# A two-layer convolution kernel on one core: ScalarE's root for the first statistics, and ScalarE's copies of the first two streams' weights placed earlier

## The chip, the cores and the metric

The kernel runs on one core of one Trainium2 chip. The metric is the device time of one execution in microseconds, the median of several runs; the runs of one kernel shown here lie within 0.3% of each other.

## The reference

The input `x` is (16, 32, 48, 48). Two residual layers follow each other; each normalises in 16 groups of two channels per image, convolves, and adds:

```python
def _gn(v, G=16, eps=1e-05):
    g = v.reshape(B_, G, C_ // G, H_, W_)
    m = jnp.mean(g, axis=(2, 3, 4), keepdims=True)
    s = jnp.var(g, axis=(2, 3, 4), keepdims=True)
    return ((g - m) / jnp.sqrt(s + eps)).reshape(v.shape)
...
x = x + _L0_conv_ref(_gn(x), L0_conv_weight, L0_conv_bias)   # 9x9, zero padding
x = x + _L1_conv_ref(_gn(x), L1_conv_weight)                 # 5x5, reflect padding
```

The 9x9 kernels of the first layer are Gaussians made from three parameters for each pair of channels (two widths and an angle): `exp(-0.5 q)` divided by its own sum over the 81 taps. The 5x5 kernels of the second layer are given.

## The kernel before, in words

**Tiling.** The 128 partitions hold 4 neighbouring image rows of 32 channels. Images go in pairs (8 pairs, `n`), and layer 1 works on quads of four images (4 quads, `qd`). Vertically both convolutions are done in transformed form: layer 1 forms 8 streams `s(i)`, linear combinations of normalised row blocks, multiplies each by its own weights `i` with TensorE (nine horizontal taps), and combines the 8 products into output rows; layer 2 does the same with 4 streams and five taps. Each float32 operand is split into two float16 parts, `hi` and `lo` for streams, `wh` and `wl` for weights, so a product is three rows of matmuls: `wh*hi`, `wh*lo`, `wl*hi` (`conv1`, lines 1454 to 1482). ScalarE makes every `hi` and `wh` by a copy (`high_half`, `high_kernel`, `high_kernel_two`), VectorE every `lo` and `wl` by a subtraction that has to wait for that copy (`low_half`, `low_kernel`).

**Order of the work.** Every engine runs a list written out by hand, in order, and engines meet through semaphores alone. On VectorE the list is `first_quad()` and what follows it, on ScalarE the calls from line 1228 on, on TensorE the calls from line 1556 on. An instruction that waits holds up everything behind it on its engine.

**The first quad.** Nothing can be multiplied until the Gaussian weights and the first statistics exist. VectorE makes the exponents (`exponents`), ScalarE takes them through `Exp` (`kernel_exponentials`, line 1174), VectorE adds blocks of them (`outer_blocks`, `all_blocks`, `tap_pairs`, `kernel_sum`) and scales the weights of stream 1 by the reciprocal of the sum (line 884). Between these steps VectorE computes 1/sqrt(var+eps) of the first four images from `vare` in its own arithmetic: a guess from the bits of the float (`first_guess`), a Newton step (`first_newton`), and a second step of higher order (`second_root`, `first_scales`), which gives the scale `gsc` and the offset `gof`. These small operations have 4 elements per partition.

Streams 1 and 2 of the first quad take a short cut: TensorE forms them from the raw `x` (`near_rows`, with three scaled identity matrices from `near_factors`), ScalarE applies scale and offset for stream 1 (`first_stream1`) and VectorE the scale for stream 2 (`first_stream2`). The other streams need the four normalised images, which ScalarE writes to `P1` (`normalise1`, two instructions an image). TensorE then goes through `FIRST_PARTS`: for each stream a part with the five taps that were "made" and a part with the four "turned" taps, mirror images of the taps of another stream. For streams 1 and 2 TensorE turns partitions itself (`turn_partitions`, line 1527) and ScalarE copies the result (`turned_kernel`); for the rest ScalarE copies (`turn_kernel`) and DMAs from SP's queue move the partitions (line 408).

**Later statistics** (`small_stats`, line 650) use ScalarE for the root: VectorE writes `vare`, ScalarE gives `std` (`standard_deviation`, line 1102), VectorE takes the reciprocal and one Newton step. ScalarE's functions live in tables that an `ACT_TABLE_LOAD` instruction brings in; the program has three, for `Sin` (line 1229), `Exp` (line 1231) and `Sqrt` (line 1278). The last stands just ahead of the `hi` copy of the last stream of the first quad (stream 6) and of the second quad's root.

Of the kernel before, what the change touches and what calls it, by code (L numbers as in the profile page):

```python
# [26 lines left out]
ALU = mybir.AluOpType  # L27
ACT = mybir.ActivationFunctionType
# [4 lines left out]
I32 = mybir.dt.int32  # L33
# [46 lines left out]
X_SCALE = 64.0  # L80
# [10 lines left out]
NF = len(OUT_FACTORS)  # L91
EPS = 1e-5
ROUND = 12582912.0
ROOT_BITS = float(0x5F3759DF + 6 * 2**23)
ROOT3 = 0.375 ** 0.5
TWO_PI = 6.2831850
SMALL = 9

# [53 lines left out]
def build(nc, x, w0, bias, w1, tables, out):  # L152
    with ExitStack() as ctx:
# [182 lines left out]
        def block1(b):  # L336
            return ker[:, :, b * P:(b + 1) * P]
# [46 lines left out]
        MARK = {}  # L384
# [53 lines left out]
        def _(dve):  # L438
# [71 lines left out]
            def outer_blocks(part):  # L510
                dve.wait_ge(exp_done, part + 1)
                at = slice(*EXP_PARTS[part])
                done(tt(slot(2)[:, at, :], block1(0)[:, at, :], block1(2)[:, at, :], ALU.add))
                MARK["outer blocks", part] = count[0]

            def all_blocks(part):
                dve.wait_ge(dve_w, MARK["outer blocks", part])
                at = slice(*EXP_PARTS[part])
                done(tt(slot(1)[:, at, :], slot(2)[:, at, :], block1(1)[:, at, :], ALU.add))
                MARK["all blocks"] = count[0]  # L520
# [77 lines left out]
            def step(ins):  # L598

                step_count[0] += 1  # L600
                ins.then_inc(first_step_done, 1)

            def step_landed():
                dve.wait_ge(first_step_done, step_count[0])
# [10 lines left out]
            def first_variance():  # L615
                dve.wait_ge(stat_mm, 1)
                step_landed()
                step(tt(var[1][:, :], STAT[1][:, QI:], msq[1][:, :], ALU.add))
                step_landed()
                step(ts(vare[1][:, :], var[1][:, :], 0.0, EPS, ALU.max, ALU.add))  # L620

            def first_guess():
                step_landed()
                step(ts(rcp[1][:, :].bitcast(I32), vare[1][:, :].bitcast(I32), -0.5, ROOT_BITS, ALU.mult, ALU.add))
                step_landed()
                step(stt(msq[1][:, :], vare[1][:, :], -0.5 / (X_SCALE * X_SCALE), rcp[1][:, :], ALU.mult, ALU.mult))

            def first_newton():
                step_landed()
                step(tt(var[1][:, :], msq[1][:, :], rcp[1][:, :], ALU.mult))  # L630
                step_landed()
                step(stt(rcp[1][:, :], var[1][:, :], 1.5, rcp[1][:, :], ALU.add, ALU.mult))

            def second_root():

                step_landed()
                step(stt(msq[1][:, :], vare[1][:, :], ROOT3 / (X_SCALE * X_SCALE), rcp[1][:, :], ALU.mult, ALU.mult))
                step_landed()
                step(tt(var[1][:, :], msq[1][:, :], rcp[1][:, :], ALU.mult))

            def first_scales():
                step_landed()
                step(stt(msq[1][:, :], var[1][:, :], -1.25 / ROOT3, var[1][:, :], ALU.add, ALU.mult))
                step_landed()
                stt(gsc[1][:, :], msq[1][:, :], 1.875, rcp[1][:, :], ALU.add, ALU.mult).then_inc(small[1], SMALL - 2)
                dve.wait_ge(small[1], SMALL - 2)
                stt(off1[:, :], first_mean, -NEAR_OFFSET, gsc[1][:, :], ALU.mult, ALU.mult).then_inc(small[1], 1)
                stt(gof[1][:, :], first_mean, -1.0, gsc[1][:, :], ALU.mult, ALU.mult).then_inc(small[1], 1)

            def small_stats(c, n):  # L650
# [10 lines left out]
                tt(var[c][:, :], ex2, msq[c][:, :], ALU.add).then_inc(small[c], 1)  # L661
                dve.wait_ge(small[c], at + 3)
                ts(vare[c][:, :], var[c][:, :], 0.0, EPS, ALU.max, ALU.add).then_inc(small[c], 1)
                dve.wait_ge(std_done[c], n + 1 if c == 2 else n)
                nc.vector.reciprocal(rcp[c][:, :], std[c][:, :]).then_inc(small[c], 1)

                dve.wait_ge(small[c], at + 5)
# [194 lines left out]
            def first_quad():  # L862
# [7 lines left out]
                outer_blocks(0)  # L870
                first_variance()
                all_blocks(0)
                first_guess()
                outer_blocks(1)
                first_newton()
                all_blocks(1)
                second_root()
                tap_pairs()
                first_scales()
                kernel_sum()  # L880
# [5 lines left out]
                kernel_scale()  # L886
                low_half(1, 0, 0)
                scaled(block1(1), "block1")
                first_stream2()
                low_kernel(1)  # L890
                made_two()
                low_half(1, 0, 1)
                low_kernel(2)
# [182 lines left out]
        def _(act):  # L1076
# [156 lines left out]
            near_factors((0,))  # L1233
            channel_sums(1, 0, range(2, 4))
            kernel_exponentials()
            near_factors((1, 2))
            opposite_rows()
            first_stream1()
            high_half(1, 0, 0)
            normalise1(0, range(2))  # L1240
            high_kernel(1)
            normalise1(0, range(2, 3))
            high_half(1, 0, 1)
            high_kernel_two()
            turned_kernel(1, 0)
            normalise1(0, range(3, 4))
            turned_kernel(1, 1)
# [26 lines left out]
            turn_kernel(5, wh)  # L1274
            high_kernel(6)
            turn_kernel(5, wl)

            nc.scalar.activation(warm[:, :], bias_c[2][:, :], ACT.Sqrt)
            high_half(1, 0, 7)
            standard_deviation(1, 1)  # L1280
            turn_kernel(6, wh)
# [339 lines left out]
```

## Time and profile before

| what | us |
|---|---|
| median of 3 runs (lowest, highest) | 244.48 (244.37, 244.97) |
| the profiled execution's own time | 244.16 |
| its span, first to last instruction | 242.4 |
| TensorE busy in the span | 232.7 (96%) |
| VectorE busy | 211.3 (87%) |
| ScalarE busy | 154.0 (64%) |
| first matmul of the convolutions starts | 19.74 |

In the profile PE is TensorE, DVE is VectorE, ACT is ScalarE and POOL is GpSimd. A row of the timeline gives start, length, engine, line and tiles, and in brackets the idle time just ahead of it with what ended it; where instructions overlap at their ends, the next one starts a little before the one ahead is listed as done. The granted clock of TensorE was 1.00 over the whole span, that is, 2.4 GHz.

### The profile page before, as it was taken

How to read it: one execution, taken by the hardware profiler on the slowest of the kernel's cores; microseconds unless marked ns; L12 is line 12 of the kernel's file. 1: busy time of each engine (PE TensorE's matmuls, PEld its weight loads, DVE VectorE, ACT ScalarE, POOL GpSimd, SP SyncE). 2: the span in 40 equal slices, each digit the busy share in tenths (PEclk: the TensorE clock that was granted, in tenths of full speed). 3: DMA queues.
4: the chain of work that ended last, by engine and by line, in shares of the span. 5: the costliest groups of instructions: out<-in, count | busy, mean ns of one | idle time of the engine just before them, and what ended most of it. 6: DMA issues, size and time to landing. Idle time of an engine off the chain costs nothing.

```text
span 242.4 us, 4154 instructions
## 1 busy us (share of the span) xinstructions
PE 232.7 (96%) x1441; PEld 144.9 (60%) x1441; DVE 211.3 (87%) x463; ACT 154.0 (64%) x330; POOL 4.4 (2%) x12
## 2 busy tenths in 40 slices
PE   5997999899999999999999999999999999999995
PEld 5854666555565665555666665556666665655554
DVE  4997999699999999999989998999997459978943
ACT  6858898999399567999537592537359003569210
POOL 1000000050000000000000000000000000000000
DMA  6980031320025000003412000062020001521123
GB/s 212 378 329 1 14 75 45 77 55 0 0 53 159 6 1 0 0 3 101 147 64 97 0 4 0 17 187 108 1 100 0 0 0 48 162 101 55 48 97 97
DMA packets 8709, 17.24 MB, mean 71 GB/s; under 512 B 3312, under 2 KB 5616, under 8 KB 8688
## 3 DMA queue, kind: packets, MB, share of 16 engines
q1 hardware_dynamic: 7712, 16.64, 20.9%
q10 hardware_dynamic: 976, 0.34, 0.6%
q8 instruction: 11, 0.18, 0.3%
q14 instruction: 10, 0.08, 0.1%
HBM read 5.57 MB, written 4.72 MB: 42 GB/s over the span
## 4 chain that ended last, share of the span: by engine, by line
PE 68%; DVE 21%; ACT 6%; issue 4%; DMA 1%; DVEq 0%; ACTq 0%
PE banks L1478 34%; PE banks L1495 33%; DVE X L796 4%; DVE lo L763 2%; DVE whl L568 2%; ACT P L1131 1%; DVE work L563 1%; DMA prm<-in_w 1%; DVE arg L507 1%; DVE s L733 1%; DVE partU L749 1%; ACT whl L1182 1%; DVE s L499 1%; ACT hi L1154 1%; ACT junk L1098 1%
## 5 line engine op out<-in xcount | busy, mean ns | idle before, releaser
L1478 PE MATMUL banks<-hi,whl 128*128 128x360 f16 (+4 forms) x576 | 99.1, 320 | 3.2 <-ACT whl L1182 1.9
L1478 PEld LDWEIGHTS banks<-hi,whl 128*128 128x128 f16 x576 | 55.9, 99 | 38.2 <-ACT whl L1182 2.5
L1478 PE MATMUL banks<-lo,whl 128*128 128x376 f16 (+4 forms) x288 | 51.6, 320 | 0.5 <-DVE lo L763 0.5
L1098 ACT ACTIVATE junk<-X 128x576 bf16<-128x576 f32 x56 | 38.1, 681 | 2.2 <-DVE X L796 0.5
L1478 PEld LDWEIGHTS banks<-lo,whl 128*128 128x128 f16 x288 | 28.0, 98 | 17.8 <-DVE lo L763 1.1
L1495 PE MATMUL banks<-lo,wh 128*128 128x384 f16 (+1 forms) x165 | 31.8, 323 | 0.0
L1495 PE MATMUL banks<-hi,wh 128*128 128x384 f16 (+1 forms) x165 | 31.8, 323 | 0.0
L1495 PE MATMUL banks<-hi,wl 128*128 128x384 f16 (+1 forms) x165 | 31.8, 323 | 0.0
L1154 ACT CAST hi<-work 128x416 f16<-128x416 f32 x32 | 16.6, 538 | 19.9 <-PE banks L1495 14.1
L1154 ACT CAST hi<-s 128x384 f16<-128x384 f32 x32 | 15.3, 508 | 17.8 <-DVE s L730 12.1
L1144 ACT ACTIVATE work<-work,gof,gsc 128x26 f32<-128x26 f32 (+1 forms) x48 | 23.3, 577 | 3.6 <-DVE gof L674 3.6
L1495 PEld LDWEIGHTS banks<-hi,wl 128*128 128x128 f16 x165 | 15.9, 97 | 10.5
L1495 PEld LDWEIGHTS banks<-lo,wh 128*128 128x128 f16 x165 | 15.9, 97 | 10.5
L1495 PEld LDWEIGHTS banks<-hi,wh 128*128 128x128 f16 x165 | 16.0, 98 | 10.4
L763 DVE TENSOR_TENSOR lo<-work,hi 128x416 f16<-128x416 f32 x32 | 17.4, 584 | 1.6 <-ACT hi L1154 1.5
L796 DVE SCALAR_TENSOR_TENSOR X<-pd,X 128x384 f32<-128x384 f32 x36 | 18.1, 558 | 0.0
L796 DVE SCALAR_TENSOR_TENSOR X<-ps,X 128x384 f32<-128x384 f32 x36 | 18.1, 558 | 0.0
L1131 ACT ACTIVATE P<-X,gof,gsc 128x336 f32<-128x336 f32 x30 | 17.7, 658 | 0.5 <-DVE gof L674 0.5
L763 DVE TENSOR_TENSOR lo<-s,hi 128x384 f16<-128x384 f32 x32 | 16.4, 552 | 0.4
L786 DVE SCALAR_TENSOR_TENSOR ps<-banks,mb 128x384 f32<-128x384 f32 x12 | 6.6, 554 | 8.3 <-PE banks L1478 7.6
L1165 ACT ACTIVATE mb<-banks,bias 128x384 f32<-128x384 f32 x12 | 6.9, 572 | 8.2 <-PE banks L1478 8.2
L1098 ACT ACTIVATION_READ_ACCUMULATOR junk<-X 128x1 f32 x56 | 10.5, 187 | 0.0
(141 smaller groups left out, 231.1 us busy)
## 6 DMA issues: line engine op xcount, KB each, us to landing
X<-in_x SPq DMA_DIRECT2D x8, 576.0 KB, 9.5
out<-X SPq DMA_DIRECT2D x7, 576.0 KB, 3.0
work<-X SPq DMA_DIRECT2D x8, 432.0 KB, 3.8
whl<-work SPq DMA_DIRECT2D x24, 64.0 KB, 2.0
work<-X SPq DMA_DIRECT2D x8, 144.0 KB, 3.6
stage<-in_w SPq DMA_DIRECT2D x1, 640.0 KB, 7.2
work<-X SPq DMA_DIRECT2D x32, 12.0 KB, 2.3
out<-X SPq DMA_DIRECT2D x1, 384.0 KB, 2.6
```

What stands on the lines that cost most here:

```text
L499: done(tt(ca[:, at, :].rearrange("p k (e o) -> p k e o", o=C), centre.unsqueeze(1).to_broadcast([P, n, NE, C]), ak[:, at, :].unsqueeze(2). ...
L568: tt(made_taps(wl, i), weight1(i), made_taps(wh, i), ALU.subtract).then_inc(wl1_done, 1)
L763: tt(lo[c][:, i, :], src, hi[c][:, i, :], ALU.subtract).then_inc(lo_done[c], 1)
L786: stt(ps[1][:, :], product1(qd, k), f, mb[1][:, :], ALU.mult, ALU.add).then_inc(mid_done[1], 1)
L796: stt(out1(qd, k), tiled1(src[1][:, :]), factors[g][i], out1(qd, k), ALU.mult, ALU.add).then_inc(out_done[1], 1)
L1098: nc.scalar.activation(waste, image(n, m), function, accum_out=sums[c][:, col:col + 1]).then_inc(sums_done[c], 1)
L1131: ins = nc.scalar.activation(dst, src, ACT.Identity, bias=gof[1][:, i:i + 1], scale=gsc[1][:, i:i + 1])
L1144: ins = nc.scalar.activation(dst[:, :, d0:d1_:ds_], src[:, :, s0:s1:ss], ACT.Identity, bias=gof[2][:, i:i + 1], scale=gsc[2][:, i:i + 1])
L1154: nc.scalar.copy(hi[c][:, i, :], src).then_inc(hi_done[c], 1)
L1165: nc.scalar.activation(mb[1][:, :], src, ACT.Identity, bias=bias_c[1 if g == 0 else 2][:, 0:1], scale=FIRST1[g]).then_inc(m_read[1], 1)
L1478: ins = nc.tensor.matmul(dst[:, :, o0:o1], w[1][:, i, t * P:(t + 1) * P], src[:, :, o0 + dx:o1 + dx], start=(first and part == 0 and t == ...
L1495: ins = nc.tensor.matmul(dst, wbuf[2][:, i, j * P:(j + 1) * P], src[:, rows, t:t + W], start=(part == 0 and t == 0), stop=(part == 2 and t ...
```

## The change

Four edits. (1) The first statistics no longer use VectorE's own root. VectorE writes `vare`, ScalarE loads the table of `Sqrt` right behind the exponentials and takes the root (`standard_deviation(1, 0)`), and VectorE does a reciprocal and one Newton step (`first_root`, `first_newton`, `first_scales`). The load that stood at line 1278 is gone, since the table stays. (2) ScalarE's copy of stream 1's weights (`high_kernel(1)`) stands behind the first normalised image instead of the second. (3) ScalarE's copies of stream 2's weights stand ahead of the third image (number 2 in the code) instead of behind it. (4) On VectorE, `low_kernel(1)` stands ahead of `first_stream2` instead of behind it. Constants of the old root go. The count that `small_stats` waits for grows by one, since the first quad now uses `std_done` too.

```diff
@@ -617,32 +615,22 @@
                 step_landed()
                 step(tt(var[1][:, :], STAT[1][:, QI:], msq[1][:, :], ALU.add))
                 step_landed()
-                step(ts(vare[1][:, :], var[1][:, :], 0.0, EPS, ALU.max, ALU.add))
-
-            def first_guess():
-                step_landed()
-                step(ts(rcp[1][:, :].bitcast(I32), vare[1][:, :].bitcast(I32), -0.5, ROOT_BITS, ALU.mult, ALU.add))
+                ts(vare[1][:, :], var[1][:, :], 0.0, EPS, ALU.max, ALU.add).then_inc(small[1], 4)
+
+            def first_root():
+                dve.wait_ge(std_done[1], 1)
+                step(nc.vector.reciprocal(rcp[1][:, :], std[1][:, :]))
                 step_landed()
                 step(stt(msq[1][:, :], vare[1][:, :], -0.5 / (X_SCALE * X_SCALE), rcp[1][:, :], ALU.mult, ALU.mult))
 
             def first_newton():
                 step_landed()
                 step(tt(var[1][:, :], msq[1][:, :], rcp[1][:, :], ALU.mult))
-                step_landed()
-                step(stt(rcp[1][:, :], var[1][:, :], 1.5, rcp[1][:, :], ALU.add, ALU.mult))
-
-            def second_root():
-
-                step_landed()
-                step(stt(msq[1][:, :], vare[1][:, :], ROOT3 / (X_SCALE * X_SCALE), rcp[1][:, :], ALU.mult, ALU.mult))
-                step_landed()
-                step(tt(var[1][:, :], msq[1][:, :], rcp[1][:, :], ALU.mult))
+                MARK["first newton"] = step_count[0]
 
             def first_scales():
-                step_landed()
-                step(stt(msq[1][:, :], var[1][:, :], -1.25 / ROOT3, var[1][:, :], ALU.add, ALU.mult))
-                step_landed()
-                stt(gsc[1][:, :], msq[1][:, :], 1.875, rcp[1][:, :], ALU.add, ALU.mult).then_inc(small[1], SMALL - 2)
+                dve.wait_ge(first_step_done, MARK["first newton"])
+                stt(gsc[1][:, :], var[1][:, :], 1.5, rcp[1][:, :], ALU.add, ALU.mult).then_inc(small[1], SMALL - 6)
                 dve.wait_ge(small[1], SMALL - 2)
                 stt(off1[:, :], first_mean, -NEAR_OFFSET, gsc[1][:, :], ALU.mult, ALU.mult).then_inc(small[1], 1)
                 stt(gof[1][:, :], first_mean, -1.0, gsc[1][:, :], ALU.mult, ALU.mult).then_inc(small[1], 1)
@@ -661,7 +649,7 @@
                 tt(var[c][:, :], ex2, msq[c][:, :], ALU.add).then_inc(small[c], 1)
                 dve.wait_ge(small[c], at + 3)
                 ts(vare[c][:, :], var[c][:, :], 0.0, EPS, ALU.max, ALU.add).then_inc(small[c], 1)
-                dve.wait_ge(std_done[c], n + 1 if c == 2 else n)
+                dve.wait_ge(std_done[c], n + 1)
                 nc.vector.reciprocal(rcp[c][:, :], std[c][:, :]).then_inc(small[c], 1)
 
                 dve.wait_ge(small[c], at + 5)
@@ -870,11 +858,10 @@
                 outer_blocks(0)
                 first_variance()
                 all_blocks(0)
-                first_guess()
                 outer_blocks(1)
+                first_root()
+                all_blocks(1)
                 first_newton()
-                all_blocks(1)
-                second_root()
                 tap_pairs()
                 first_scales()
                 kernel_sum()
@@ -886,8 +873,8 @@
                 kernel_scale()
                 low_half(1, 0, 0)
                 scaled(block1(1), "block1")
+                low_kernel(1)
                 first_stream2()
-                low_kernel(1)
                 made_two()
                 low_half(1, 0, 1)
                 low_kernel(2)
@@ -1233,15 +1220,18 @@
             near_factors((0,))
             channel_sums(1, 0, range(2, 4))
             kernel_exponentials()
+            nc.scalar.activation(warm[:, :], bias_c[2][:, :], ACT.Sqrt)
+            standard_deviation(1, 0)
             near_factors((1, 2))
             opposite_rows()
             first_stream1()
             high_half(1, 0, 0)
-            normalise1(0, range(2))
+            normalise1(0, range(1))
             high_kernel(1)
-            normalise1(0, range(2, 3))
+            normalise1(0, range(1, 2))
             high_half(1, 0, 1)
             high_kernel_two()
+            normalise1(0, range(2, 3))
             turned_kernel(1, 0)
             normalise1(0, range(3, 4))
             turned_kernel(1, 1)
@@ -1274,8 +1264,6 @@
             turn_kernel(5, wh)
             high_kernel(6)
             turn_kernel(5, wl)
-
-            nc.scalar.activation(warm[:, :], bias_c[2][:, :], ACT.Sqrt)
             high_half(1, 0, 7)
             standard_deviation(1, 1)
             turn_kernel(6, wh)
```

How the instructions stand on the engines, at the three places that matter, is shown here; names as in the program (`arg` holds the exponentials, `s_1` the streams of layer 1, `whl` both halves of layer 1's weights, `P` the normalised images).

ScalarE, from the end of the exponentials to stream 2's weights; before:

```order
L1178 ACTIVATE arg<-arg 128x768
L1110 ACTIVATE factors<-tab 128x128 x2
L1199 CAST opposite<-tab 128x128
L1118 ACTIVATE s_1<-banks,off,gsc 128x2x48 x4
L1154 CAST hi<-s_1 128x384
L1131 ACTIVATE P<-X,gof,gsc 128x7x48 x4
L1182 CAST whl<-work 128x640
L1131 ACTIVATE P<-X,gof,gsc 128x7x48 x2
L1154 CAST hi<-s_1 128x384
L1188 CAST whl<-work 128x384
```

and with the change:

```order
L1165 ACTIVATE arg<-arg 128x768
L1223 ACT_TABLE_LOAD
L1223 ACTIVATE warm<-bias 128x1
L1091 ACTIVATE std<-vare 128x4
L1097 ACTIVATE factors<-tab 128x128 x2
L1186 CAST opposite<-tab 128x128
L1105 ACTIVATE s_1<-banks,off,gsc 128x2x48 x4
L1141 CAST hi<-s_1 128x384
L1118 ACTIVATE P<-X,gof,gsc 128x7x48 x2
L1169 CAST whl<-work 128x640
L1118 ACTIVATE P<-X,gof,gsc 128x7x48 x2
L1141 CAST hi<-s_1 128x384
```

A load, a one-element `Sqrt` and the root stand ahead of the factors; the copy of stream 1's weights stands between the first and the second image, and the third image (two of these `P` instructions) is no longer ahead of stream 2's `hi`.

VectorE, the root between the block sums; before:

```order
L519 TENSOR_TENSOR work<-work,arg 128x384
L624 TENSOR_SCALAR rcp<-vare 128x4
L626 SCALAR_TENSOR_TENSOR msq<-vare,rcp 128x4
L513 TENSOR_TENSOR work<-arg 128x256
L630 TENSOR_TENSOR var<-msq,rcp 128x4
L632 SCALAR_TENSOR_TENSOR rcp<-var,rcp 128x4
L519 TENSOR_TENSOR work<-work,arg 128x256
L637 SCALAR_TENSOR_TENSOR msq<-vare,rcp 128x4
L639 TENSOR_TENSOR var<-msq,rcp 128x4
L524 TENSOR_TENSOR work<-work 128x256
L643 SCALAR_TENSOR_TENSOR msq<-var 128x4
L645 SCALAR_TENSOR_TENSOR gsc<-msq,rcp 128x4
```

and with the change:

```order
L517 TENSOR_TENSOR work<-work,arg 128x384
L511 TENSOR_TENSOR work<-arg 128x256
L622 RECIPROCAL rcp<-std 128x4
L624 SCALAR_TENSOR_TENSOR msq<-vare,rcp 128x4
L517 TENSOR_TENSOR work<-work,arg 128x256
L628 TENSOR_TENSOR var<-msq,rcp 128x4
L522 TENSOR_TENSOR work<-work 128x256
L633 SCALAR_TENSOR_TENSOR gsc<-var,rcp 128x4
```

Eight small operations have become four, and the first of the four reads `std`, which ScalarE writes.

VectorE, where stream 1's `wl` and stream 2 are made (`s_1<-banks` is `first_stream2`); before:

```order
L551 TENSOR_TENSOR arg<-arg,rs 128x5x128
L699 TENSOR_TENSOR s_1<-banks,gsc 128x192 x2
L568 TENSOR_TENSOR whl<-work,whl 128x640
L559 SCALAR_TENSOR_TENSOR work<-arg,work 128x384
L559 SCALAR_TENSOR_TENSOR work<-arg,work 128x256
```

and with the change:

```order
L549 TENSOR_TENSOR arg<-arg,rs 128x5x128
L566 TENSOR_TENSOR whl<-work,whl 128x640
L687 TENSOR_TENSOR s_1<-banks,gsc 128x192 x2
L557 SCALAR_TENSOR_TENSOR work<-arg,work 128x384
L557 SCALAR_TENSOR_TENSOR work<-arg,work 128x256
```

The subtraction that gives stream 1's `wl`, which waits for ScalarE's copy, now stands ahead of stream 2.

## Rows read from the trace of the kernel before

**Rows 1.** The chain of work that ended last: share of the span by engine.
```profile
PE 68%; DVE 21%; ACT 6%; issue 4%; DMA 1%; DVEq 0%; ACTq 0%
```
**Rows 2.** Busy time by stretch: length, busy us (instructions) by engine, clock, DMA share, GB/s.
```profile
24.30:46.80 22.50, 22.50 (x144) 13.83 (x142) 20.84 (x37) 20.70 (x42) 0.00 (x0) 1.00 0.20 48
...
79.00:240.00 161.00, 160.70 (x1020) 98.82 (x1020) 140.77 (x310) 89.39 (x194) 0.00 (x0) 1.00 0.16 53
```
**Rows 3.** What TensorE waited for from 0 to 75 us: total, times, longest.
```profile
PE banks L1478 <- ACT whl L1182: 1.9, 1, 1.9
PE banks L1478 <- ACT hi L1154: 1.2, 2, 0.9
PE banks L1478 <- DVE lo L763: 0.5, 1, 0.5
```
**Rows 4.** Timeline of ScalarE from 9.5 us: start, length, instruction, idle before it.
```profile
9.59 1.90 ACT L1178 ACTIVATE arg<-arg 128x1152 f32<-128x1152 f32 x2 [0.54 <-DVE arg L507]
11.40 0.49 ACT L1110 ACTIVATE factors<-tab 128x128 f32<-128x128 f32 x2
...
14.89 1.40 ACT L1118 ACTIVATE s<-banks,off,gsc 128x96 f32<-128x96 f32 x4 [2.81 <-DVE gof L648]
```
**Rows 5.** Timeline of ScalarE: the table loads of `Exp` and of `Sqrt`.
```profile
3.86 1.28 ACT L1231 ACT_TABLE_LOAD   x1
...
45.65 1.28 ACT L1278 ACT_TABLE_LOAD   x1
```
**Rows 6.** Timeline of VectorE, 11.7 to 17 us: variance, a block sum, scales, first weights.
```profile
11.74 0.17 DVE L620 TENSOR_SCALAR vare<-var 128x4 f32<-128x4 f32 x1
...
12.56 0.42 DVE L513 TENSOR_TENSOR work<-arg 128x256 f32<-128x256 f32 x1
...
14.36 0.16 DVE L645 SCALAR_TENSOR_TENSOR gsc<-msq,rcp 128x4 f32<-128x4 f32 x1
...
14.64 0.15 DVE L648 SCALAR_TENSOR_TENSOR gof<-mom,gsc 128x4 f32<-128x4 f32 x1
...
16.16 0.82 DVE L884 SCALAR_TENSOR_TENSOR work<-work,krec 128x640 f32<-128x640 f32 x1
```
**Rows 7.** Timeline of ScalarE, 16.7 to 23 us: images, weights, turned copy.
```profile
16.74 2.34 ACT L1131 ACTIVATE P<-X,gof,gsc 128x336 f32<-128x336 f32 x4
18.98 0.71 ACT L1182 CAST whl<-work 128x640 f16<-128x640 f32 x1
...
21.13 0.81 ACT L1188 CAST whl<-work 128x384 f16<-128x384 f32 x2
22.58 0.59 ACT L1207 CAST whl<-banks 128x512 f16<-128x512 f32 x1 [0.64 <-PE banks L1533]
```
**Rows 8.** Timeline of VectorE, 18 to 25 us: stream 2, stream 1's `wl`, first use of `P`.
```profile
18.19 0.61 DVE L699 TENSOR_TENSOR s<-banks,gsc 128x192 f32<-128x192 f32 x2
19.72 0.83 DVE L568 TENSOR_TENSOR whl<-work,whl 128x640 f16<-128x640 f32 x1 [0.92 <-ACT whl L1182]
...
24.32 0.56 DVE L705 TENSOR_TENSOR partA<-P 128x384 f32<-128x384 f32 x1 [0.79 <-ACT P L1131]
```
**Rows 9.** Timeline of ScalarE behind the load of `Sqrt`: last `hi`, second quad's root.
```profile
47.05 0.49 ACT L1154 CAST hi<-s 128x384 f16<-128x384 f32 x1
47.45 0.20 ACT L1104 ACTIVATE std<-vare 128x4 f32<-128x4 f32 x1
```
**Rows 10.** Timeline of VectorE, 45 to 49 us: last stream of quad 0, statistics of quad 1.
```profile
45.02 0.55 DVE L736 SCALAR_TENSOR_TENSOR s<-partA 128x384 f32<-128x384 f32 x1
...
46.14 0.17 DVE L663 TENSOR_SCALAR vare<-var 128x4 f32<-128x4 f32 x1
47.69 0.18 DVE L665 RECIPROCAL rcp<-std 128x4 f32<-128x4 f32 x1 [1.38 <-ACT std L1104]
...
48.49 0.16 DVE L674 SCALAR_TENSOR_TENSOR gof<-mom,gsc 128x4 f32<-128x4 f32 x1
```
**Rows 11.** Timeline of TensorE: last matmuls of the raw sums for stream 2.
```profile
15.13 2.74 PE L1442 MATMUL banks<-X,factors 128*128 128x384 f32 x8
```

More of the change, by code:

```diff
@@ L93 @@
 ROUND = 12582912.0
-ROOT_BITS = float(0x5F3759DF + 6 * 2**23)
-ROOT3 = 0.375 ** 0.5
 TWO_PI = 6.2831850
```

## The prediction

> **What bounds the kernel now.** I read the chain of waits first: TensorE holds 68% of it, VectorE 21% and ScalarE 6% [rows 1]. The busy time by stretch then tells where TensorE is the limit. From 79 us to the end it is busy for 160.70 of 161.00 us at the full clock [rows 2], so whatever moves that stretch moves the end by as much. Ahead of 79 us TensorE waits only a few times [rows 3]: 1.9 us for stream 1's weight copy, just before its first convolution at 19.74, then for `hi` and for `lo` (0.9 and 0.5 us) near 47 to 49 us. In between, from 24.3 to 46.8, it is busy all the time (22.50 of 22.50) but so nearly are VectorE (20.84) and ScalarE (20.70) [rows 2]. So an earlier start of TensorE alone is not the answer; the question is by how much the relay of ScalarE and VectorE arrives earlier at 49 us, since from there it runs on without slack until TensorE takes over at 79.
>
> The relay has two places that the change touches. Near 24 us VectorE waits 0.79 us for the fourth normalised image [rows 8]: that sets when it starts on the streams that need `P1`. Near 46 us VectorE waits 1.38 us for the second quad's root [rows 10], because ScalarE is loading the table of `Sqrt` for 1.28 us [rows 5] and then does a `hi` copy first [rows 9].
>
> **The change, part by part.**
>
> *The early load and root.* The exponentials end at 9.59+1.90 = 11.49 [rows 4]. A load took 1.28 us both times [rows 5], so it ends at 12.80; the one-element `Sqrt` takes the 0.12 us that lie between load and next instruction at 46.93 to 47.05 [rows 5, 9], and the root its 0.20 us [rows 9]: `std` lands at 13.12. `vare` is there at 11.91 [rows 6], so the root waits for nothing else. VectorE's reciprocal starts 0.04 us after `std` lands, as at 47.69 against 47.65 [rows 9, 10], at 13.16. VectorE gets there earlier: its second block sum starts at 12.56 at the latest and takes 0.42 [rows 6], so it idles at least 0.18 us and, as the two small operations ahead of the sum are gone, rather 0.46. From the reciprocal on I lay the steps at the distances of the same operations in the trace (0.2 us from a small step to one that reads it, about 0.33 for a block sum put between): product 13.37, block sum 13.45 to 13.87, Newton step 13.78, pair sum 13.90, `gsc` 14.24. `gof` followed `gsc` by 0.28 us [rows 6], so it starts at 14.52 against 14.64: **0.12 us earlier**. Eight small operations became four; the wait eats most of that. The factors that follow on ScalarE move from 11.40 to 13.03 and end near 13.5 [rows 4]; TensorE reads them at 15.13 [rows 11], so this is hidden.
>
> The price that the trace of before doesn't show is the root's landing *in this place*. Lower end: `std` is there when VectorE arrives, which gives 0.46 us back. Upper end: something as long as the load again stands behind it, 1.28 us more. I take the plain load, since it has the same length in both rows, and 47.05 follows 46.93 with only the small `Sqrt` between.
>
> *The order of the images and weights.* `first_stream1` then starts at 14.77 instead of 14.89 [rows 4], and the first image at 16.74-0.12 = 16.62 [rows 7]. Two of the four `P` instructions take half of 18.98-16.74, 1.12 us, so stream 1's weight copy starts at 17.74 and lands at 18.45 (its weights are scaled by 16.98 even before [rows 6]). TensorE starts at 18.50, 1.24 us earlier. Now VectorE's side: `low_kernel(1)` waits for that copy, starts at 18.48 (it waited 0.92 us before [rows 8] and has that wait now too), and behind it, 0.74 us later, `first_stream2` runs from 19.22 to 19.83 instead of from 18.19 [rows 8]. ScalarE has done the second image by 18.36+1.12 = 19.48 and finds stream 2 missing: a **new wait of 0.39 us**, and 0.06 us more until stream 2's weights are made. Against this, ScalarE's 0.64 us of waiting for TensorE's turned partitions [rows 7] is gone: TensorE now turns them near 21.2, and the third image stands ahead of that copy. The net is -0.12 -0.64 +0.45 = -0.31, and with the copies and images laid out one by one (18.36 second image, 19.87 `hi`, 20.33 weights of stream 2, 21.05 third image, 22.17 turned copy, 22.65 fourth image until 23.87) VectorE's first use of `P` comes at 23.92 instead of 24.32: I take **-0.40 us**. Bounds: -0.85 with no new wait, and nothing at all if the new wait is twice as long.
>
> *TensorE's 1.24 us at the start* are mostly given back: its next streams wait for `hi` and `lo` that come only 0.40 us sooner. I cost this part at nothing beyond the 0.40.
>
> *The load that is gone near 46 us.* ScalarE's load starts at 45.65 [rows 5], when the turned copy ahead of it is done; the stream that `hi` reads is ready at 45.02+0.55 = 45.57 [rows 10]. Without the load `hi` runs from 45.65 to 46.14, ahead of the need, and the root starts when `vare` lands at 46.14+0.17 = 46.31 [rows 10], at 46.35 instead of 47.45 [rows 9]: **-1.10 us** for `std`, `gof` and the `lo` and `wl` queued behind them on VectorE. What is late next is VectorE's own row of small steps, which is part of the chain already. TensorE's wait for `hi` shrinks to nothing, the one for `lo` stays.
>
> *The sum:* -0.40 -1.10 = -1.50 us, carried by the relay to 79 us and by TensorE to the end. The profiled execution took 244.16, so 242.66; the median of the runs is 0.32 us above it, which puts the forecast at **243.0**.
>
> **A rule against it.** Both rows show 1.28 us for a load and the next instruction right behind it [rows 5, 9]. The Trainium skill, "ScalarE: Activation LUTs", section "What ACT_TABLE_LOAD costs", gives the same 1283 ns for the load but adds a drain of about 1380 ns to every switch, and advises to batch by set. By that page, as an estimate, the switch in the middle of the root's chain would hold `gof` up by some 1.4 us and leave a gain near 0.1 us; the rows of the loads here don't show the drain.
>
> **The rivals.**
>
> 1. *The root comes late.* VectorE stands in its wait for `std`, and behind that wait are the block sums, stream 1's weights and all that follows; each us costs one us. A stretch as long as the load (1.28, the only row for such a thing) leaves 1.50-1.28 = 0.22: 244.3, no change. For it: no load in this trace stands in a chain like this one. Against: [rows 5, 9]. The page above is of this kind.
> 2. *Loads come back: slower.* The table of `Sqrt` now stays in for the factor copies, the casts and the normalising, where `Exp`'s stood before. If any of these called for another table, a load would stand ahead of it and one more ahead of the next root: two loads of 1.28 in the chain, -1.50+2.56 = +1.06, 245.5. It turns the sign as soon as more than 1.50 us come in, and shows as slower from 2.2 on. Against: after 45.65 the same kinds of instruction run behind `Sqrt`'s table in the trace of before, and the order of the changed kernel has three loads as before.
> 3. *The early start carries.* If TensorE, busy throughout from 24.3 to 46.8 [rows 2], were the true clock of that stretch, its 1.24 us would arrive, and with the 1.4 us of load and small `Sqrt` (45.65 to 47.05) the gain would be 2.6: 241.9. Against: VectorE and ScalarE are busy 92% of it too, and TensorE's waits at its end are for them.
> 4. *The gain of 46 us is lost behind it,* at a transfer of turned weights or another wait that the relay hides now; only the 0.40 stays: 244.1, no change. Against: nothing between 49 and 79 us has a clock of its own, the images and weights having been loaded long before.
>
> **How the numbers follow.** About 0.3%, 0.73 us, is what a measurement can tell from no change. Forecast 0.76 (its own range 242.5 to 243.5: the 0.85 and nothing for the front, and some tenths of scatter), rival 1 0.06, rival 2 0.04, rival 3 0.08, rival 4 0.06. Faster is the forecast and rival 3, 0.84; the same is rivals 1 and 4, 0.12; slower is rival 2, 0.04. For 8 in 10 the range takes the milder half of rivals 3 and 4 in: 242.2 to 243.9.
>
> **What would show it.** In the profile after: three loads, the last near 11.5 us with 1.28 us; VectorE's reciprocal near 13.2 after an idle of about 0.4; `gof` near 14.5; TensorE's first convolution near 18.5; a wait of ScalarE for stream 2 of about 0.4 near 19.5, and no longer one for turned partitions; the first use of `P` near 23.9; the second quad's reciprocal near 46.2 with an idle of some 0.2 instead of 1.38; TensorE's third row of stream 6 and all after it 1.5 us earlier. It would be wrong if the reciprocal came after 14, if TensorE stood idle between 49 and 79 by as much as it gains, or if the front moved by more than 0.9.

## The result, and the profile after

The changed kernel takes **242.79 us** (median of 4 runs, 242.66 to 243.21) against 244.46 for the kernel before in the same session (244.37 to 244.97): a ratio of 0.993, 95% interval 0.9912 to 0.9949, or 1.67 us less. The forecast was 243.0. The profiled execution took 242.82 with a span of 241.0, against 244.16 and 242.4.

One thing has to be known to read its times: in this execution the second pair of images landed later than in the profile of before, and the exponentials on ScalarE ended at 11.69 instead of 11.49. ScalarE's steps behind them, up to the first use of the normalised images near 24 us, are shifted by these 0.2 us. The timeline of ScalarE after the change (start, length, instruction, idle before it):

```profile
8.26 0.68 ACT L1085 ACTIVATE junk<-X 128x576 bf16<-128x576 f32 x1 [0.67 <-DMA X<-in_x]
...
9.81 1.88 ACT L1165 ACTIVATE arg<-arg 128x1152 f32<-128x1152 f32 x2
11.71 1.28 ACT L1223 ACT_TABLE_LOAD   x1
13.00 0.20 ACT L1223 ACTIVATE warm<-bias 128x1 f32<-128x1 f32 x1
13.11 0.19 ACT L1091 ACTIVATE std<-vare 128x4 f32<-128x4 f32 x1
...
14.95 1.40 ACT L1105 ACTIVATE s<-banks,off,gsc 128x96 f32<-128x96 f32 x4 [1.06 <-DVE gof L636]
...
16.79 1.22 ACT L1118 ACTIVATE P<-X,gof,gsc 128x336 f32<-128x336 f32 x2
17.92 0.71 ACT L1169 CAST whl<-work 128x640 f16<-128x640 f32 x1
...
20.05 0.51 ACT L1141 CAST hi<-s 128x384 f16<-128x384 f32 x1 [0.30 <-DVE s L687]
20.52 0.82 ACT L1175 CAST whl<-work 128x384 f16<-128x384 f32 x2
...
22.37 0.56 ACT L1194 CAST whl<-banks 128x512 f16<-128x512 f32 x1
```

The load takes 1.28 us and nothing follows it but the small `Sqrt` and the root [rows 5]. The weights of stream 1 come 1.06 us sooner [rows 7], the new wait for stream 2 is there (0.30 us), and the old wait for TensorE's turned partitions is gone. VectorE in the same stretch:

```profile
12.49 0.42 DVE L511 TENSOR_TENSOR work<-arg 128x256 f32<-128x256 f32 x1
13.33 0.18 DVE L622 RECIPROCAL rcp<-std 128x4 f32<-128x4 f32 x1 [0.42 <-ACT std L1091]
...
14.69 0.16 DVE L636 SCALAR_TENSOR_TENSOR gof<-mom,gsc 128x4 f32<-128x4 f32 x1
...
18.66 0.82 DVE L566 TENSOR_TENSOR whl<-work,whl 128x640 f16<-128x640 f32 x1 [0.34 <-ACT whl L1169]
19.40 0.62 DVE L687 TENSOR_TENSOR s<-banks,gsc 128x192 f32<-128x192 f32 x2
...
24.09 0.56 DVE L693 TENSOR_TENSOR partA<-P 128x384 f32<-128x384 f32 x1 [1.16 <-ACT P L1118]
```

VectorE waits 0.42 us for the root; its first use of the normalised images comes at 24.09 instead of 24.32 [rows 8]. Near 46 us, ScalarE and then VectorE:

```profile
45.37 0.51 ACT L1141 CAST hi<-s 128x384 f16<-128x384 f32 x1
46.12 0.20 ACT L1091 ACTIVATE std<-vare 128x4 f32<-128x4 f32 x1 [0.23 <-DVE vare L651]
```

```profile
45.91 0.17 DVE L651 TENSOR_SCALAR vare<-var 128x4 f32<-128x4 f32 x1
46.35 0.18 DVE L653 RECIPROCAL rcp<-std 128x4 f32<-128x4 f32 x1 [0.27 <-ACT std L1091]
...
47.15 0.16 DVE L662 SCALAR_TENSOR_TENSOR gof<-mom,gsc 128x4 f32<-128x4 f32 x1
```

The roles have turned round: ScalarE now waits for `vare` instead of VectorE for the load, and `gof` comes at 47.15 instead of 48.49 [rows 10], 1.34 us earlier: 0.23 us are there at the first use of the images, and 1.11 come between that and `gof`. From there on nothing is lost: the profiled execution is 1.34 us shorter too (242.82 against 244.16), and TensorE is busy for 160.82 of the 161 us from 77.5 on, as it was from 79 [rows 2]. What TensorE waits for up to 80 us, without its first wait for the tables (3.0 us before and after):

```profile
PE banks L1466 <- ACT hi L1141: 0.7, 2, 0.4
PE banks L1466 <- DVE lo L751: 0.5, 1, 0.5
PE banks L1405 <- ACT junk L1085: 0.2, 1, 0.2
PE banks L1466 <- ACT whl L1169: 0.2, 1, 0.2
```

Its wait for stream 1's weights has fallen from 1.9 to 0.2 us [rows 3], but only 1.06 of this is the weights: the rest is that its raw sums came 0.59 us later in this execution than in the profile of before [rows 11]. Of the waits for `hi`, the 0.9 us near 47 is gone, 0.34 near 56 stands in both profiles, and one of 0.37 is new, in which TensorE gives back a part of its earlier start:

```profile
15.72 2.74 PE L1430 MATMUL banks<-X,factors 128*128 128x384 f32 x8
...
35.40 0.95 PE L1466 MATMUL banks<-hi,whl 128*128 128x384 f16 x5 [0.37 <-ACT hi L1141]
```

### The profile page after: what moved, and what is told of

The parts are those of the page before. It is cut to its first block, busy times and chain, and to the rows that moved or that the text cites. A ratio compares the mean times of both kernels' runs of the same rounds, so it can differ in the third digit from the quotient of the medians.

```text
span 241.0 us, 4153 instructions
## 1 busy us (share of the span) xinstructions
PE 233.4 (97%) x1441; PEld 145.2 (60%) x1441; DVE 211.1 (88%) x459; ACT 154.1 (64%) x331; POOL 4.4 (2%) x12
## 4 chain that ended last, share of the span: by engine, by line
PE 68%; DVE 18%; ACT 6%; issue 4%; DMA 3%; SPq 0%; DVEq 0%; ACTq 0%
PE banks L1466 34%; PE banks L1483 33%; DVE X L784 4%; DMA X<-in_x 3%; DVE lo L751 2%; DVE whl L566 2%; ACT junk L1085 1%; ACT P L1118 1%; DVE work L561 1%; DVE s L721 1%; DVE partU L737 1%; ACT arg L1165 1%; DVE s L724 1%; DVE s L730 1%; ACT s L1105 1%
## 5 line engine op out<-in xcount | busy, mean ns | idle before, releaser
L1483 PEld LDWEIGHTS banks<-hi,wh 128*128 128x128 f16 x165 | 16.0, 98 | 10.4
```

The lines of the kernel that those rows point to most:

```text
L1483: ins = nc.tensor.matmul(dst, wbuf[2][:, i, j * P:(j + 1) * P], src[:, rows, t:t + W], start=(part == 0 and t == 0), stop=(part == 2 and t ...
```

## The experiments

**First set: the parts alone.** Theory: the load's new place is worth 1.10, the shorter root 0.12, the order 0.28. Rivals: the front does it all, or TensorE's early start does.

*Only the load moved* (kernel before):

```diff
             kernel_exponentials()
+            nc.scalar.activation(warm[:, :], bias_c[2][:, :], ACT.Sqrt)
...
-            nc.scalar.activation(warm[:, :], bias_c[2][:, :], ACT.Sqrt)
             high_half(1, 0, 7)
```

> The kernel before, with one edit: the one-element Sqrt, and with it the load of its table, stands right behind the exponentials, where ScalarE waited 2.81 us anyway. Root and order stay as they were. Theory: the load in the way at 46 us costs 1.10 us of the relay, and 11.5 to 13 us is free room on ScalarE, so 244.46 - 1.10 = 243.35; the second quad's reciprocal starts about 0.04 us after std, near 46.4, with an idle of about 0.25. Rival: the gain comes from the front (root and order) and the stall at 46 us is taken up by the next wait: 244.4.

Measured 243.90 against 244.39 (ratio 0.9973, 0.9961 to 0.9984): less than both the theory and all of the change. But its profile does what was expected at the second quad's reciprocal, where the idle is 0.27:

```profile
47.71 0.18 DVE L665 RECIPROCAL rcp<-std 128x4 f32<-128x4 f32 x1 [0.27 <-ACT std L1104]
```

From VectorE's first use of the images (25.46) to `gof` of the second quad (48.52) it takes 23.06 us, as in the changed kernel, against 24.17 before: the load's 1.11 us is there. What differs is at the front, where VectorE's mean of the first images (`mom`) came at 11.55 instead of 10.42, after a wait for TensorE:

```profile
11.55 0.56 DVE L611 TENSOR_REDUCE mom<-banks 128x4 f32<-128x384 f32 x1 [1.03 <-PE banks L1426]
```

Nothing of the edit stands ahead of 11.5 us. TensorE's busy time in two stretches, in this run and then in the profile of before (length, busy us with instructions, granted clock, DMA share, GB/s):

```profile
7.00:8.00 1.00, 1.00 (x5) 1.00 0.98 384
8.00:9.00 1.00, 1.00 (x5) 1.00 0.99 393
```

```profile
7.00:8.00 1.00, 1.00 (x8) 1.00 0.96 348
8.00:9.00 1.00, 1.00 (x8) 1.00 1.00 393
```

The same matmuls (the plain sums of the first images) start 0.32 us apart in the first of these and 0.16 us apart in the second; the counts in brackets take in matmuls that only reach into the stretch. That is a factor of two, as between 1.2 and 2.4 GHz. The column of the granted clock says 1.00 in both, but neither trace holds a record of the clock. The trace of the changed kernel does: its record begins at 6.97 us, where the spacing of these matmuls halves too. So the 1.00 ahead of that moment is no reading, and the 2.4 GHz told above for the whole span of the kernel before is borne out only from 6.0 us on. TensorE had been running its idle matmuls since 2.97 us in the profile of before and since 3.00 in this one; the faster rate began near 6.0 and near 9.2. So the start of the kernel differs by up to 1.1 us between executions (an execution in which the rate doubles late is called late from here on), about as much as the times of the kernel before spread in this set (244.11 to 245.35). Why the twelve runs of this kernel came late more often than the 23 of the kernel before stays open.

*Only root and load* (changed kernel, order as before):

```diff
-            normalise1(0, range(1))
+            normalise1(0, range(2))
             high_kernel(1)
-            normalise1(0, range(1, 2))
+            normalise1(0, range(2, 3))
             high_half(1, 0, 1)
             high_kernel_two()
-            normalise1(0, range(2, 3))
...
-                low_kernel(1)
                 first_stream2()
+                low_kernel(1)
```

> The changed kernel with ScalarE's images and weights and VectorE's low_kernel(1) back in the order of before: only the root and its load are changed. Theory: the load's 1.10 us and 0.12 us of the root, 244.46 - 1.22 = 243.25, so within 0.15 us of the run that only moves the load. Rival: the shorter root is worth more than the 0.12, because VectorE has four small steps fewer: 242.8, all of the change.

Measured 242.95, ratio 0.9937 (0.9922 to 0.9953): 0.3 us beyond the theory and nearer to the rival. Its profile, of the slowest of its runs (243.53), offers a reason. The mean came 0.85 us late (11.27), yet `gof` stands at 14.90, only 0.26 us behind [rows 6]: VectorE would have waited for ScalarE's root anyway. This hides a part of a late clock, not all of it. ScalarE now waits for TensorE's late raw sums,

```profile
15.36 1.40 ACT L1105 ACTIVATE s<-banks,off,gsc 128x96 f32<-128x96 f32 x4 [1.60 <-PE banks L1429]
```

and the first use of the images comes at 24.79, 0.47 us later than before. VectorE's own root hands a late clock on in full: from the mean to the first use it is 13.90 us in the profile of before and 13.91 with the load moved alone, where the mean was 1.13 us late. That this makes the 0.3 us is a fit to one profile, not shown.

*Only the order* (kernel before, with the order edits of the diff):

> The kernel before with the order edits alone (stream 1's weights behind the first image, stream 2's weights ahead of the third, low_kernel(1) ahead of first_stream2). Theory: TensorE starts 1.1 us earlier, the relay only about 0.3 us, so 244.46 - 0.3 = 244.2. Rival: TensorE's early start carries to the end: 243.4.

Measured 244.28 against 244.39, ratio 0.999 (0.9978 to 1.0003): 0.1 us where the theory has 0.3. The interval, from 0.5 us faster to 0.1 slower, has room for the theory and none for the 1.1 us of TensorE's early start: it does not carry.

*Stream 2 ahead of the low weights again* (changed kernel):

```diff
-                low_kernel(1)
                 first_stream2()
+                low_kernel(1)
```

> The changed kernel with one edit undone: first_stream2 ahead of low_kernel(1) on VectorE, as before. Theory: ScalarE's wait for stream 2 (0.30 us) and most of the next one go, so the fourth image and the relay come about 0.4 us earlier: 242.79 - 0.4 = 242.4, faster than both kernels. TensorE's third row of stream 1 doesn't wait, since wl is there by 19.6 and wanted at 20.3. Rival: the low weights come late for TensorE and the gain is lost, 242.8 or more.

Measured 242.89, ratio 0.993 (0.991 to 0.995): 242.4 was expected, and there is no gain over the changed kernel that can be told. In its profile the clock came up somewhat late too (mean at 10.80); stream 2 waited for TensorE's raw sums and ScalarE for the weights made behind it. VectorE, then ScalarE:

```profile
18.76 0.62 DVE L687 TENSOR_TENSOR s<-banks,gsc 128x192 f32<-128x192 f32 x2 [0.60 <-PE banks L1430]
```

```profile
20.62 0.82 ACT L1175 CAST whl<-work 128x384 f16<-128x384 f32 x2 [0.51 <-DVE work L557]
```

**Second set: the same with TensorE busy from 1 us on.** To take the scatter out, TensorE's idle matmuls no longer wait for the tables but take zeros that VectorE writes first:

```diff
+            nc.vector.memset(warming_zeros[:, :], 0.0).then_inc(zeros_set, 1)
             first_quad()
...
             def warming(n):
                 for _ in range(n):
-                    nc.tensor.matmul(banks[:, 6, 0:P], group_t, group_t, start=True, stop=True)
-
+                    nc.tensor.matmul(banks[:, 6, 0:P], warming_zeros[:, :], warming_zeros[:, :], start=True, stop=True)
+
+            pe.wait_ge(zeros_set, 1)
+            warming(WARMING)
             pe.wait_ge(tab_loaded, 16)
-            warming(WARMING)
```

with nine of them instead of six. The four kernels are those named before; the diffs of the parts are the ones above.

> The kernel before with one addition: TensorE's idle matmuls at the start take zeros that VectorE sets at once, nine instead of six, so they begin near 1 us instead of 2.97 and don't wait for the tables. In the profiles so far the plain sums of the first images ran at one matmul per 0.28 us for a while and then at one per 0.14 (TensorE's two clocks), and the change came at about 5.9 us in the profile of before and as late as 9.2 in another run; VectorE's mean of the first images came up to 1.1 us later for it. Theory: begun earlier, the clock is up sooner, VectorE's first reduction comes near 10.4 in each run and the spread of the times (244.1 to 245.3 for the kernel before) narrows to its lower end: 244.1. Rival: the spread comes from the input's transfers: 244.4 with the same spread.

> The changed kernel with the same early matmuls. Theory: the sum of the prediction, 1.50 us, is what stands between this one and the kernel before with early matmuls: 242.6; VectorE idles about 0.45 us at the root. The plain comparison gave more (1.67) because VectorE's wait for the root hides a late clock that the old root passes on. Rival: the gain is 1.67 here too.

> The changed kernel with early matmuls, and first_stream2 ahead of low_kernel(1) as before. Theory: without early matmuls this edit gained nothing because TensorE's raw sums for stream 2 ended at 18.7 instead of 17.9 and first_stream2 waited for them (0.60 us); with the clock up in time it starts near 18.3, ScalarE's waits for stream 2 and its weights shrink from 0.4 us to nearly nothing, and the time is 0.3 to 0.4 us below the one beside it: 242.2. Rival: the weights of stream 2 come late all the same, since they are queued behind low_kernel(1): no difference.

> The kernel before with early matmuls and the load of Sqrt's table moved behind the exponentials, root and order as before. Theory: 1.10 us below the kernel before with early matmuls: 243.0. Without early matmuls the gain was 0.65, and its profile had the clock come up at 9.2 us and VectorE's reduction 1.1 us late. Rival: the load's move is worth 0.65 only, something behind 49 us takes the rest: 243.45.

The first of these expectations puts the matmuls at one per 0.28 and 0.14 us; the traces have them 0.32 and 0.16 us apart.

The times fall into groups now. Most executions of each kernel agree within 0.25 us, the narrow group; in the rest (five of twelve runs of the kernel before, two of seven with stream 2 first) the time is 1.4 to 1.9 us higher. Both profiles that fell among these have the low rate until past 9 us. So the early matmuls do not end the scatter, and where they fail the time is worse than any without them (up to 245.95 for the kernel before, against 245.35).

The traces show one thing that goes with it. The nine idle matmuls end at 5.26 us, and TensorE then stands idle until the first images have landed; the changed kernel, then the kernel before:

```profile
5.58 4.42 PE L1418 MATMUL banks<-X,tab 128*128 128x192 f32 x24 [0.32 <-DMA X<-in_x]
```

```profile
6.10 5.78 PE L1430 MATMUL banks<-X,tab 128*128 128x192 f32 x24 [0.84 <-DMA X<-in_x]
```

In the seven profiles with early matmuls (this set and the next) this idle is 0.32 to 0.43 us in the three where the rate had doubled by 7.0 us, and 0.53 to 0.87 in the four where it doubled past 9. No run changes the idle alone, and without early matmuls the rate came late with no such idle, so this is not shown to be the cause. The landing of the first images by itself is too little: it differs by 0.6 us at most, the mean by 1.8.

| with early matmuls | median of the narrow group, us | against the first |
|---|---|---|
| kernel before | 244.24 (7 of 12 runs) | |
| load moved alone | 243.20 (5 of 5) | -1.04 (expected -1.10) |
| changed kernel | 242.70 (5 of 5) | -1.54 (expected -1.50) |
| changed, stream 2 first | 242.26 (5 of 7) | -1.98 (expected -1.9) |

Taken over all runs, the differences are -1.07, -1.57 and -2.01. So the load is two thirds of the gain, and the fourth edit of the change costs 0.44 us: with the clock up in time, the order `first_stream2`, `low_kernel(1)` is the better one. Of this only the time is shown: the profile of that kernel fell among the late executions, so the waits that should shrink were not seen.

**Third set: prices and rivals.** These runs are of another session than the second set (the kernel before, without early matmuls, took 244.23 us here and 244.35 there), so a difference across the two sets holds to about 0.1 us.

*Two more loads ahead of the root* (changed kernel, early matmuls):

```diff
-            nc.scalar.activation(warm[:, :], bias_c[2][:, :], ACT.Sqrt)
+            nc.scalar.activation(warm[:, 0:1], bias_c[2][:, :], ACT.Sqrt)
+            nc.scalar.activation(warm[:, 1:2], bias_c[2][:, :], ACT.Exp)
+            nc.scalar.activation(warm[:, 2:3], bias_c[2][:, :], ACT.Sqrt)
             standard_deviation(1, 0)
```

> The changed kernel with early matmuls and two more table loads in front of the root (Sqrt, Exp, Sqrt, each of one element, into places of their own). Theory: every load costs its 1.28 us and 0.12 for the small instruction and nothing behind it, and a later root costs one for one: 2.8 us on top of 242.7, 245.5; VectorE idles 3.2 us at the reciprocal instead of 0.36. Rival, a drain of about 1.4 us at each switch as the notes on ScalarE have it: 248.3. Rival, part of the root's delay is hidden: 244.5.

Measured 245.73, 3.03 us above the changed kernel with early matmuls, and slower than the kernel before (ratio 1.0056, 1.0043 to 1.0069). ScalarE:

```profile
11.59 1.28 ACT L1226 ACT_TABLE_LOAD   x1
12.88 0.20 ACT L1226 ACTIVATE warm<-bias 128x1 f32<-128x1 f32 x1
13.09 1.28 ACT L1227 ACT_TABLE_LOAD   x1
14.38 0.20 ACT L1227 ACTIVATE warm<-bias 128x1 f32<-128x1 f32 x1
14.59 1.28 ACT L1228 ACT_TABLE_LOAD   x1
```

A switch costs 1.50 us from load to load (1.28, 0.20, and 0.02 between): no drain, and the rival with one (248.3) is out. The root's delay is paid one for one: VectorE's first use of the images comes 15.42 us behind the end of the exponentials, against 12.40 in the changed kernel. The theory was 0.2 us short, as a small instruction ahead of another load costs 0.22 us and not 0.12. So the prediction's slower rival had the price of a load right (1.28), and only its condition (loads that come back) did not hold. In this execution the mean came at 12.29, after 1.71 us of waiting for TensorE, so VectorE's idle at the reciprocal was 1.56 us and not the 3.2 expected; the 15.42 leaves no room for a delay by the mean: behind loads as long as these a late clock costs nothing.

*TensorE started late* (changed kernel, early matmuls):

```diff
                     if bank in held:
                         pe.wait_ge(*held[bank])
+                    if i == 1:
+                        pe.wait_ge(wl1_done, 1)
```

> The changed kernel with early matmuls; TensorE's first convolution waits for stream 1's low weights as well, so it starts near 19.4 instead of 18.6. Nothing else is changed. Theory: the early start of TensorE is given back at its next waits anyway, so the time stays at 242.7, and its later waits for hi shrink. Rival (the early start carries): 243.5.

Measured 242.67, against 242.70 without the wait. TensorE's first convolution started at 19.22 instead of 18.56, after a wait of 0.83 us for the low weights, and nothing came of it:

```profile
PE banks L1469 <- DVE whl L568: 0.8, 1, 0.8
```

*GpSimd for the fourth image* (stream 2 first, with and without early matmuls):

```diff
+            normalise_last(0)
             normalise_last(1)
...
-            normalise1(0, range(3, 4))
```

> The best so far (early matmuls, first_stream2 ahead of low_kernel(1)), and GpSimd normalises the fourth image of the first quad as it already does for the second quad, where its two instructions took 3.52 us. Theory: ScalarE's relay is 1.22 us shorter, VectorE's first use of P comes when VectorE is free, near 22.7 instead of 23.6, less some tenths that VectorE's steps lose beside GpSimd (1.75 us for three row updates beside it, 1.49 without): 242.25 - 0.8 = 241.5. Rival: VectorE slows down so much between 14.7 and 18.2, with the kernel's sum and stream 1's weights in it, that nothing is left: 242.3 or more.

> The same without the early matmuls: the changed kernel, first_stream2 ahead of low_kernel(1), GpSimd for the fourth image. Theory: some tenths more than with early matmuls, as TensorE's clock comes up later: 241.9, below both kernels. Rival: no better than the changed kernel, 242.8.

Measured 241.79 with early matmuls (241.5 expected; ratio to the kernel before 0.9918, 0.9892 to 0.9943) and 242.53 without (241.9 expected; 0.9923, 0.991 to 0.9936). Both are below the kernel before; the first, 0.9 us below the changed kernel with early matmuls, is the best version of this study, with two of its six runs at 243.18 and 243.61; the profile, of the first of these, has the late clock. The gain over its neighbour is 0.47 us where 0.8 was expected. In both profiles VectorE no longer waits for the images at all but comes to them straight from the weights, so VectorE is the bound there, in late executions at least; the one with early matmuls:

```profile
23.50 0.82 DVE L551 TENSOR_TENSOR arg<-arg,rs 128x640 f32<-128x640 f32 x1
24.23 0.55 DVE L695 TENSOR_TENSOR partA<-P 128x384 f32<-128x384 f32 x1
```

(Both profiles are of late executions, whence the times.)

**All profiles together.** Set side by side, the fourteen profiles say more than any one of them. Some of them (us):

| profiled execution | its time | first use of `P` | `gof` of the second quad |
|---|---|---|---|
| kernel before | 244.16 | 24.32 | 48.49 |
| order alone | 244.00 | 24.18 | 48.34 |
| load moved alone | 244.17 | 25.46 | 48.52 |
| root and load alone | 243.53 | 24.79 | 47.86 |
| changed kernel | 242.82 | 24.09 | 47.15 |
| two more loads | 245.74 | 26.99 | 50.05 |

In all fourteen the time is 195.65 to 195.72 us above the start of that `gof`. So nothing behind it takes or gives anything, whatever TensorE gained at its start. From the first use of `P` to that `gof` it is 24.16 to 24.17 us in the three with the load near 46, and 23.05 to 23.07 in the nine without it where ScalarE makes all four images (23.22 and 23.23 in the two with GpSimd's): the load's place is worth 1.10 to 1.11 us in every profile, early clock or late. All the rest, the scatter too, is settled ahead of 27 us.

## Why the prediction was right

- *The root*: `std` was forecast for 13.12, 1.63 us behind the exponentials' end at 11.49; it landed at 13.30, 1.61 us behind 11.69. The reciprocal followed it 0.03 us later, with an idle of 0.42 where some 0.46 was forecast; `gof` starts 1.36 us behind the reciprocal, as forecast. This step held to 0.02 us. The drain of some 1.4 us at each switch, which the Trainium skill gives ("ScalarE: Activation LUTs", section "What ACT_TABLE_LOAD costs"), shows neither here nor in the run with two more loads, where a switch takes 1.50 us with its small instruction; the page's 1283 ns for the load itself agrees with the 1.28 of every row.
- *The order*: forecast were a wait of 0.39 us for stream 2 and 0.06 for its weights; it shows 0.30 and 0.06. The first use of `P` was forecast 12.43 us behind the exponentials (23.92) and came 12.40 behind them (24.09). TensorE's start, 18.50 forecast, was 18.69, again the 0.2 of the inputs.
- *TensorE's early start costed at nothing*: the run that starts it 0.66 us later has the same time. The prediction had its waits for `hi` shrink to nothing; the 0.9 us near 47 did, but the smaller one near 56 was left out, and a new one at 35.40 is where a part of the start goes back.
- *The load near 46*: -1.10 forecast for the reciprocal's wait; the idle went from 1.38 to 0.27, 1.11 us less, every profile has this 1.11 us, and alone with early matmuls the move gave 1.04.
- *The sum*: -1.50, and -1.54 where TensorE's clock is up early in both kernels: the load's 1.11 and so, as an estimate, 0.43 for the front, forecast at 0.40. The two profiles differ by 1.34, of which 0.23 is the front, with the inputs 0.2 us later. The plain runs gave -1.67. What these have beyond the sum fits what the root-only run shows, a late clock hidden in part behind the wait for ScalarE, which the prediction did not know of; as it is a tenth of a per cent, the runs don't prove it. That the median came out below the 243.0 forecast is to that extent luck.
- *The rivals*: a late root and loads that come back did not happen, though the price of a load was right; the early start does not carry; nothing behind the second quad's `gof` took the gain.

## What to carry to other kernels

A table load belongs where its engine waits anyway; moved from the middle of a relay into such a place it gave back its full 1.1 us, and a short chain on another engine can then use the function at once. Before an instruction that waits for another engine is placed, look at what is queued behind it: the low weights, which wait for ScalarE's copy, were put ahead of stream 2, and that order cost 0.44 us of the 1.98 that were to be had. An early start of the busiest engine was worth nothing here, as its next inputs came from a relay that had not moved. And where single executions scatter, compare them at landmarks: two starts in each trace told the load's 1.11 us from the scatter, which the medians of plain runs did not.

## What was not expected of the hardware

TensorE's plain sums run at half the rate for the first microseconds, and the moment of the change differs from execution to execution (6.0 to 10.4 us), though the profile's clock column reads 1.00 throughout. Starting the idle matmuls 1.9 us sooner narrows the times of most executions to 0.25 us but leaves some at the late moment. GpSimd normalised its image in 1.38 us at 16 us into the run with early matmuls, where the two same instructions took 3.51 in the second quad of the same execution; what VectorE does at the same time differs in the two places, but no run here shows that this is the cause:

```profile
16.05 1.38 POOL L1383 TENSOR_SCALAR P<-X,gsc,gof 128x336 f32<-128x336 f32 x2 [14.62 <-DVE gof L638]
47.78 3.51 POOL L1383 TENSOR_SCALAR P<-X,gsc,gof 128x336 f32<-128x336 f32 x2 [30.36 <-DVE gof L664]
```
